# Channel order of x from the split of d on: reloads and stores of 128 partitions, taps of u in two pieces

## The reference, cut to what matters

```
gn(x)   : group norm, 32 groups of 4 neighbouring channels
t1      = einsum('nchw,he->ncew', gn(x), p1)
t3      = depthwise conv of t1 with p3 (9 x 9)
t4      = grouped conv of t3 with p4 (4 channels in, 5 x 1)      # called d below
t5      = einsum('ncew,ewf->ncf', t4, p5)                        # f = 3 * channel + k, 384 of them
t6      = conv of t5 along f with p6 (3 taps)                    # called u below
x1      = x + einsum('ncf,nfp->ncp', t6, rows k-1, k, k+1 of gn(x)) / sqrt(3 * 128)
y       = conv_w (128 x 512) times [gn(x1), three upsampled Haar details of gn(x1)]
out     = x1 + relu(batchnorm(y) * gamma + beta)
```

## Time and profile before

| what | us |
|---|---|
| median of 3 runs (388.44 to 389.29) | 388.76 |
| the profiled execution's own time | 385.7 |
| its span, first to last instruction | 383.8 |
| DVE / POOL / ACT busy | 318.9 / 257.7 / 242.4 |
| PE busy (ends are modelled) | 299.0 |
| mean granted clock of PE, 1 is 2.4 GHz | 0.911 |

### The profile page before, as it was taken

One profiled execution on the slowest core, in us unless ns is written; L12 is line 12 of the kernel. 1 busy time (PEld: TensorE's weight loads), 2 busy tenths in 40 slices (PEclk: granted clock), 3 DMA queues, 4 the chain that ended last, 5 costly groups with the idle time before them and its releaser, 6 DMA issues.

```text
span 383.8 us, 5224 instructions
## 1 busy us (share of the span) xinstructions
PE 299.0 (78%) x1679; PEld 245.7 (64%) x1679; DVE 318.9 (83%) x537; ACT 242.4 (63%) x377; POOL 257.7 (67%) x284
## 2 busy tenths in 40 slices
PE   0698646999999999488999999999999998720000
PEld 0254421999998996376888888888888886510000
DVE  1899967699998975989779999999999998597920
ACT  2389996476667668945666666666666665308910
POOL 9634464699998794386688888888888888520000
PEclk9999995699999999789999999999999999885555
DMA  8999910000243137999900000000000000004998
GB/s 175 172 203 210 192 41 1 3 0 2 52 103 82 42 77 153 218 216 214 191 3 2 2 1 2 0 1 2 0 3 0 2 0 1 2 0 120 261 260 233
DMA packets 19630, 31.07 MB, mean 81 GB/s; under 512 B 5300, under 2 KB 13236, under 8 KB 19604
## 3 DMA queue, kind: packets, MB, share of 16 engines
q1 hardware_dynamic: 19412, 30.33, 35.9%
q0 software_dynamic: 192, 0.42, 0.5%
HBM read 17.89 MB, written 8.39 MB: 68 GB/s over the span
## 4 chain that ended last, share of the span: by engine, by line
POOL 30%; ACT 19%; DVE 17%; PE 15%; issue 10%; DMA 2%; SPq 2%; DVEq 0%; POOLq 0%; ACTq 0%
POOL g_lo L472 9%; POOL g_lo L445 9%; PE wide L765 7%; ACT y_sb L640 6%; DVE x_sb L1103 4%; DVE d_split L967 4%; ACT t_hi L496 3%; DVE s_lo L916 3%; POOL rs L456 2%; POOL rs L453 2%; ACT t_f L502 2%; ACT toe L507 2%; POOL rs L454 2%; DMA p_raw<-in_p 2%; POOL s_f L415 2%
## 5 line engine op out<-in xcount | busy, mean ns | idle before, releaser
L415 POOL TENSOR_TENSOR s_f<-toe,ci_mask 128x640 f32<-128x640 f32 x32 | 40.9, 1277 | 14.9 <-DVE s_lo L918 14.9
L639 ACT ACTIVATE g_hi<-x_sb,rs 128x1024 fp32r<-128x1024 f32 x16 | 21.5, 1342 | 45.7 <-POOL rs L457 43.8
L472 POOL TENSOR_TENSOR g_lo<-y_sb,g_hi 128x1024 fp32r<-128x1024 f32 x15 | 36.0, 2401 | 12.6 <-ACT y_sb L640 12.6
L898 DVE STREAM_TRANSPOSE xa<-x_ring 128x1024 f32<-128x1024 f32 x16 | 32.1, 2008 | 8.4 <-DMA x_ring<-in_x 8.1
L231 PE MATMUL wide<-g_hi,t_hi 128*128 128x512 f32 x96 | 38.9, 406 | 0.1
L916 DVE TENSOR_TENSOR s_lo<-s_f,s_hi 128x640 fp32r<-128x640 f32 x32 | 35.0, 1092 | 4.8 <-ACT s_hi L522 4.8
L233 PE MATMUL wide<-g_hi,t_lo 128*128 128x512 f32 x96 | 37.9, 395 | 0.0
L232 PE MATMUL wide<-g_lo,t_hi 128*128 128x512 f32 x96 | 37.8, 394 | 0.0
L445 POOL TENSOR_TENSOR g_lo<-y_sb,g_hi 128x1024 fp32r<-128x1024 f32 x15 | 35.9, 2395 | 0.9 <-ACT g_hi L609 0.9
L380 POOL TENSOR_TENSOR t_lo<-t_f,t_hi 128x512 fp32r<-128x512 f32 x10 | 15.8, 1578 | 21.4 <-ACT t_f L502 21.4
L521 ACT CAST s_hi<-s_f 128x640 fp32r<-128x640 f32 x32 | 23.3, 729 | 10.2 <-POOL s_f L418 10.2
(11 more groups left out here) (174 smaller groups left out, 988.0 us busy)
## 6 DMA issues: line engine op xcount, KB each, us to landing
x_ring<-in_x SPq DMA_DIRECT2D x32, 256.0 KB, 5.9
x_sb<-in_x SPq DMA_DIRECT2D x32, 256.0 KB, 13.5
out<-x_sb SPq DMA_DIRECT2D x28, 256.0 KB, 4.0
d_sb<-t_out SPq DMA_DIRECT2D x58, 68.0 KB, 2.1
out<-x_sb SPq DMA_DIRECT2D x8, 128.0 KB, 2.3
p_raw<-in_p SPq DMA_DIRECT2D x8, 96.0 KB, 8.1
d_sb<-t_out POOLq DMA_DIRECT2D x6, 68.0 KB, 5.4
w_raw<-in_conv_w SPq DMA_DIRECT2D x4, 64.0 KB, 5.5
```

Source lines behind the costliest of these rows:

```text
L415: pool.tensor_tensor(s3_f[:, g % 2], toe3[:, g].unsqueeze(2).broadcast_to([128, SHIFTS, CI, E]), ci_mask[:, :].unsqueeze(1).unsqueeze(3).b ...
L472: pool.tensor_tensor(g2_lo[:, :], y_sb[:, n, :], g2_hi[:, :].bitcast(F32), ALU.subtract).then_inc(s["g2_lo"], 1)
L898: dve.transpose(xa[:, n % 2], x_ring[:, n // 2 % XR, n % 2, :].rearrange("p (h w) -> p w h", w=W)).then_inc(s["xa"], 1)
```

## The change

- From the split of d on, channels are in the order of x. `d_sb` is [jc, b, ci, g in batch, image], and the shuffles write it with the same blocks as before. The split reads it with g innermost (a step of 17 elements, as before) and writes `d_split` with a step of 4 elements, where it wrote 8 neighbours in a row. Each entry of `SPLITS` becomes four instructions, one per jc, on ACT, DVE and POOL; the signal comes after the fourth.
- The reloads of x and the stores are one DMA of 128 partitions each (8 for 32, and 9 for 36).
- conv_w, p6, gamma and beta are loaded in one DMA each (4 for 16); `w_perm` and ACT's copy into it are gone. ACT's four p5 copies write k-major and read with a step of 3 elements for 12.
- The tap terms of u have two pieces (256 and 127 columns) for three.
- A second averaging matrix `g_from` turns quarters into x order where the statistics of the first pass are averaged; `g_mean` is now block diagonal. POOL builds both in the first microseconds: one memset and two selects more.

```
-        d_sb = put("d_sb", [JC, C, NO])
+        d_sb = put("d_sb", [JC, NB, CI, GB, NO])
...
-        def split_views(b, n0, n1):
-
-            def pick(v):
-                return v.rearrange("p n j (co g) -> p n (j co) g", co=CI)[:, :, :, GB * b:GB * b + GB]
-            return (pick(d_sb[:, :, :, n0:n1].rearrange("p j c n -> p n j c")),
-                    pick(d_split[:, n0:n1, 0]), pick(d_split[:, n0:n1, 1]))
+        def split_views(b, n0, n1, jc):
+
+            def pick(part):
+                v = d_split[:, n0:n1, part, jc, 4 * GB * b:4 * GB * b + 4 * GB]
+                return v.rearrange("p n (g co) -> p n co g", co=CI)
+            return d_sb[:, jc, b, :, :, n0:n1].rearrange("p co g n -> p n co g"), pick(0), pick(1)
+        def reload_x(eng, k):
+            eng.dma_start(x_sb[:, 2 * k:2 * k + 2, :],
+                          x[2 * k:2 * k + 2].rearrange("n c h w -> c n (h w)")).then_inc(x_in[k], 16)
...
+                sp.dma_start(out[n:end].rearrange("n c h w -> c n (h w)"),
+                             x_sb[:, n:end, :]).then_inc(s["stored"], 16)
...
             def t4_low(i):
                 b, n0, n1, _ = SPLITS[i]
                 pool.wait_ge(s["d_hi"], i + 1)
-                src, hi, lo = split_views(b, n0, n1)
-                pool.tensor_tensor(lo, src, hi.bitcast(F32), ALU.subtract).then_inc(s["d_lo_pool"], 1)
+                for jc in range(JC):
+                    src, hi, lo = split_views(b, n0, n1, jc)
+                    ins = pool.tensor_tensor(lo, src, hi.bitcast(F32), ALU.subtract)
+                ins.then_inc(s["d_lo_pool"], 1)
...
-                        act.wait_ge(s["w_in"], 16 * CI)
-                        act.copy(w_perm[:, :, :].rearrange("p k (c g) -> p k c g", c=CI),
-                                 w_raw[:, :].rearrange("p (k g c) -> p k c g", k=4, c=CI)).then_inc(s["w_pm"], 1)
...
-                    act.copy(p5_sb[:, n - P5_AT, :].rearrange("p (k c g) -> p k c g", k=3, c=CI),
-                             p5_raw[:, n - P5_AT, :].rearrange("p (g c k) -> p k c g", c=CI, k=3)
+                    act.copy(p5_sb[:, n - P5_AT, :].rearrange("p (k c) -> p k c", k=3),
+                             p5_raw[:, n - P5_AT, :].rearrange("p (c k) -> p k c", k=3)
...
                 dve.wait_ge(s["u_act"], k + 1)
-                for to, n, frm in ((C, 2 * C, 0), (G, 3 * G, 2 * C), (1, G - 1, 3 * C - G)):
+                for to, n, frm in ((C, 2 * C, 0), (1, C - 1, 2 * C)):
...
-                for to, n, frm in ((0, 2 * C, C), (2 * C, 3 * G, G), (3 * C - G, G - 1, 1)):
+                for to, n, frm in ((0, 2 * C, C), (2 * C, C - 1, 1)):
```

More of the change, by code:

```diff
@@ L144, in build @@
         cursor[0] = at_s3
-        w_perm = put("w_perm", [4, C])
         one_s3 = 4 * SHIFTS * CI * E
@@ L292, in _ @@
                 load_x(sp, x_ring[:, k % XR], k)
[L293 to L309, removed]
+                if k == 2:
+                    sp.dma_start(w_raw[:, :], conv_w).then_inc(s["w_in"], 16)
+                elif k == 3:
+                    for r in range(2 * JL):
+                        sp.dma_start(p5_raw[16 * r:16 * r + 16, :, :],
+                                     p5.rearrange("e (j r) o f -> r e j (o f)", r=2 * JL)[r + 1 - 2 * (r % 2)]
+                                     ).then_inc(s["p5_in"], 16)
+                elif k == 5:
+                    sp.dma_start(p6_sb[:, :], p6.rearrange("c a b d -> c (a b d)")).then_inc(s["p6_in"], 16)
+                    sp.dma_start(gb[:, 0:1], gamma.rearrange("(c a) -> c a", a=1),
+                                 allow_slow_non_contiguous=True).then_inc(s["p6_in"], 16)
+                    sp.dma_start(gb[:, 1:2], beta.rearrange("(c a) -> c a", a=1),
+                                 allow_slow_non_contiguous=True).then_inc(s["p6_in"], 16)
             for b in range(NB):
@@ L323, in _ @@
                     sp.wait_ge(s["t5"], 3)
-                load_x(sp, x_sb[:, 2 * k:2 * k + 2, :], k)
+                reload_x(sp, k)
             for n, end in STORES:
                 sp.wait_ge(s["res"], end + 1)
[L327 to L330, removed]
+                sp.dma_start(out[n:end].rearrange("n c h w -> c n (h w)"),
+                             x_sb[:, n:end, :]).then_inc(s["stored"], 16)
+            sp.wait_ge(s["stored"], 16 * len(STORES))
         @block.gpsimd
@@ L585, in _ @@
                     wait_d(act)
-                src, hi, _ = split_views(b, n0, n1)
-                act.copy(hi, src).then_inc(s["d_hi"], 1)
+                for jc in range(JC):
+                    src, hi, _ = split_views(b, n0, n1, jc)
+                    ins = act.copy(hi, src)
+                ins.then_inc(s["d_hi"], 1)
             def middle_of_u(k):
@@ L965, in _ @@
                     dve.wait_ge(s["d_hi"], i + 1)
-                    src, hi, lo = split_views(b, n0, n1)
-                    dve.tensor_tensor(lo, src, hi.bitcast(F32), ALU.subtract).then_inc(s["d_lo"], 1)
+                    for jc in range(JC):
+                        src, hi, lo = split_views(b, n0, n1, jc)
+                        ins = dve.tensor_tensor(lo, src, hi.bitcast(F32), ALU.subtract)
+                    ins.then_inc(s["d_lo"], 1)
             def u_views(k):
```

32 lines of the change are left out of this document (18 added, 14 removed).

## The result

| | before | changed |
|---|---|---|
| median, us | 388.99 (388.44 to 389.29, 4 runs) | 384.54 (384.31 to 386.18, 4 runs) |
| span of the profiled execution | 383.8 | 384.4 |
| ratio | | 0.9896, 95% interval 0.9866 to 0.9927 |

A forecast was written before the change was run, and what follows sets the result against it. Bounds: ACT's chain in the first pass, the split's DVE/POOL race, a POOL-ACT ring in the loop, stores in the tail. -0.9 - 0.6 + 6.8 + 0.7 - 9.8 = -3.8: 381.9 profiled, 385.0 median; range 378.0 to 389.0.

The forecast's parts named there:

- signs of being wrong: First product starting near 163, an image loop pass of 10.3 us or more, or a tail staying at 260 GB/s.
- Stores, -9.8: Tail: one DMA of 128 partitions stores at 400 GB/s for 261, gaining 9.8 us.
- First pass, -1.5: First pass, on ACT's chain: `w_perm` goes, -0.9 us, and p5 copies with a smaller step, -0.6.
- ACT's split: Split of d: cutting in four adds 0.24 us per entry, the step in writes nothing; POOL's start moves to 161.3.
- DVE's split: Split of d: three strided operands make a whole batch 4.8 us for 3.9.
- POOL's quarter, 1.5 (1.3 to 1.7): Split of d: each of POOL's four instructions takes 1.5 us, the upper bound being a third more.
- The race, +6.8 and +0.7: Split: DVE and POOL alternate, delaying PE's t5 products, +6.8 us; then POOL's second `t4_low` gates ACT's p5 cast, +0.7.
- Taps, 0: Image loop: two tap pieces may save DVE 0.15 us twice per image, but gain 0, covered by POOL's ring.
- Rival 4: Image loop: shorter taps bring `u_mean` ahead of POOL's norm factor; POOL waits 0.5 us in 13 passes, +6.5; chance 0.07.
- the ring: Image loop: chain of waits through POOL and ACT (low parts, norm factors, normalising), taken to set the 9.96 us pass.
- I carry the difference over: Whole kernel: the median's 3.1 us above the profiled execution is added to the forecast of 381.9, giving 385.0.
- Reload, 0: Reload of x: eight DMAs for 32 end some 15 us sooner, but ACT never waits for an image, so 0.

The follow-up runs named there:

- the chunk experiment: Kernel before with each piece of the split of d cut into four instructions on ACT, DVE and POOL, old channel order: 389.85 us, ratio 1.0085.
- again: The changed kernel, unchanged, measured and profiled in another series of runs: 384.39 us, ratio 0.9963 to the kernel before.

## Why the prediction came near, and where it was wrong

The number was right; the sum behind it was not, so that it came within half a microsecond is luck. The profiled execution of the changed kernel was forecast at 381.9 and took 386.18, 4.3 more. Two errors cancelled. One of the prediction's own signs of being wrong also showed: a pass took 10.3 or more.

**Stores, -9.8: right.** -10.2 in the ledger, and +10.0 when the stores alone were turned back. The 400 GB/s chosen stood at 402 to 404. The Trainium skill, "SBUF — State Buffer", in its summary, puts transfers with HBM at about 358 GB/s; the trace does not agree, with 402 to 404 GB/s over 10 us. Its section "Door 1: The DMA port swizzle" gives 218 GB/s for 32 or 64 partitions and 436 for 128. The whole, at 404, lies below its bound; stores in quarters (256 to 306 GB/s by their order) and halves (up to 345) lie above theirs, so for DMAs that follow each other in a queue the traces do not agree with it.

**First pass, -1.5: right.** In the chain of waits `w_perm` is gone (0.91) and the p5 copies are links of 0.52 to 0.61 for 0.67 to 0.76, 0.6 in all; the first convolution starts 1.3 sooner. The ledger's -2.2 is in part scatter: the stage's end lies at 144.6 to 146.3 in the six profiled executions with the old first pass and at 143.5 to 144.1 in the eight with the new, means 145.3 and 143.7, so -1.6. **ACT's split** was right to a tenth: POOL could start at 159.72, forecast 161.3 less the 1.5. The step in ACT's writes cost nothing seen; the reason given for that, that reads and writes overlap, no run tests. **DVE's split** was put too high, 4.8 for a batch: it took 4.3. (The row it was read from gives 2.3 ns per element with its fixed cost, 1166 ns for 512, not 2.1; the batch took 2.0.)

**POOL's quarter, 1.5 (1.3 to 1.7): the term that failed on size.** It is 1.9, outside the bounds. "A third more, an estimate" had no row behind it; the chunk experiment shows 0.57 us for the step alone.

**The race, +6.8 and +0.7: right size (+6.6), in part by another way.** "All four POOL instructions go ahead of the fourth" did not happen. DVE's short instructions stood one behind the other, and POOL did not get between them; the fifth `d_lo` came at 160.9, not at 167.3 (168.8 less 1.5). The turns hit the sixth. So the first product was not late, the second was, by 4.5 and not by 6.8. Behind it came 2.0 and not 0.7. There the prediction had the second product follow the first at once and put nothing for a low clock, but PE stood idle for 3.60 us between them and the second began at 0.50; and it had POOL gate ACT's cast of p5, which in fact did not wait for POOL. That POOL's second `t4_low` meets `u_mean` was right. What the sum had no term for is the second chain: POOL's own work, two `t4_low` of 8.6 and 7.4 for 5.65 and 5.10, ends only 1.9 us before the cast of p5, which may not start without it, so the second product 4.2 us sooner won nothing.

**Taps, 0: wrong, the largest miss.** Rival 4 had the mechanism, the place and nearly the price (+6.5 for 13 passes; 12 passes of 0.46 make +5.5, and 5.0 was measured in medians), with a chance of 0.07. It failed on its condition: it asked for `u_mean` ahead of the factor, and set a margin of 0.18 against a saving of 0.15. Counted from the end of POOL's low part of g ahead of it, the factor starts after 2.26 us in every one of these kernels (medians of the passes) and `u_mean` after 2.45 with three pieces and 2.33 with two. So the saving was 0.12 (that of `u_previous` is lost in L1039's wait for POOL), `u_mean` still starts 0.06 after the factor, and the factor is shut out all the same: the margin had to stay above something between 0.06 and 0.19. And the cover was named wrongly: "DVE is not in the ring" says nothing of a DVE instruction that shuts out one of POOL's in the ring.

**"I carry the difference over": wrong, the error that cancelled.** The 3.1 us between median and profiled execution were taken for an offset that both kernels have. But that execution was a fast one: it had the lucky outcome of the race, worth 2.3. And the changed kernel's profiled execution was a slow one, with a 15th pass of 10.10 us where the others of this kernel and its variants have 8.13 to 8.67. Taken from all profiled executions, the changed kernel against the kernel before with the unlucky outcome comes to -1.6 for the first stage, +2.7 for the split (45.0 for 42.3), +5.4 for the 14 passes and -10.5 for the tail (26.2 for 36.7), -4.0 in all; with the lucky outcome the split costs +5.9 and the sum is -0.8. The three comparisons with the changed kernel's time (this one, "again", and the reload in quarters) gave -4.5, -1.7 and -4.1. The rest of the spread is in part the granted clock, as in the 15th pass; how it is shared wasn't traced.

**Reload, 0: right**, 384.32 for 384.4 to 384.5.

## What to carry to other kernels

Where an engine's instruction shuts another's out, shortening the first can lengthen the second: compare the new start times pair by pair, above all where a margin is a few tenths of a microsecond and one of the two is in a ring. Starts need not change places for that. Before a difference is taken from one profiled execution, see whether a race in it can fall two ways and where its granted clock was low, and give a stage's cost for either. Where two chains end within 2 us of each other, price both: moving one alone can win nothing. And move DMAs of all partitions at once; where the layout forbids it, at least order the pieces so that neighbours in the queue lie in opposite halves.

## What the runs showed of the hardware that was not expected

- POOL pays for a step in its other operands, DVE hardly: a subtraction of 448 elements per partition took POOL 1.33 us with a step in one operand and 1.9 with one in all three (4.2 ns per element), DVE 0.93 in the latter case. In the split as a whole DVE's instructions of 544 elements went from 1.00 to 1.07.
- With DVE's instructions back to back a POOL instruction waited 1.0 us through all of them (2.94 us for 1.9), and once DVE had waited for something else, they took turns one for one. The same program fell either way in different executions.
- A POOL instruction of one element per partition took 0.71 us for 0.27 when a DVE instruction of 0.59 started 0.06 us after it, and 0.27 when that started 0.19 after it.
- One DMA of 128 partitions stored at 402 to 404 GB/s, two of 64 at 250 to 345, four of 32 at 256 to 265, and four of 32 in the order 0, 2, 1, 3 at 287 to 306, all with the DMA engines busy 0.84 or more.
